# The first loads, the attention mask and the end of attention in a one-core network kernel: three edits at once

## The chip, the cores and the metric

The kernel runs on one core of a Trainium2 chip. The metric is the device time of one execution in microseconds, the median over the runs made. TensorE (PE) multiplies, VectorE (DVE), ScalarE (ACT) and GpSimd (POOL) do elementwise work, SyncE (SP) only issues transfers; ACT and POOL issue some as well. The engines run their own lists of instructions in order and meet at semaphores.

## The reference, cut to what matters

The input is x, 64 sequences of 64 tokens with 256 features, and one type (0 to 2) per sequence.

```python
def gated(x, wi0, wi1, wo): return gelu(x @ wi0) * (x @ wi1) @ wo       # 256 -> 1024 -> 256
# first network: a shared one and one chosen by type, mixed by a gate per sequence
y = mix(gated(x, Wi0[t], Wi1[t], Wo[t]), gated(x, sWi0, sWi1, sWo))
x = x + attention(y, 16 heads of 16, causal, softmax) @ Wo + bo
# second network: three shared relu networks, two experts by type, mixed by a gate of four
z = mix(experts(x), relu(x @ s0) @ t0, relu(x @ s1) @ t1, relu(x @ s2) @ t2)
x = x + moe(z)      # router of three layers, top 2 of 8 experts with a capacity
```

## The kernel before, in words

Every float32 product is split: data and weights are each held as a float16 high part and a float16 low part, and three float16 matmuls (high by high, high by low, low by high) add up to the product. So each matrix that is used must be loaded, scaled to a high part by ACT (`first_weights`, `weight_high`) and to a low part by DVE, and so must each piece of x (`x_group`).

The stages follow one another: the shared gated network `cs` (4 iterations of 16 steps), the typed gated network `ce`, attention over 16 chunks of 256 tokens, three shared relu networks `es[0]` to `es[2]`, the experts `ee`, the router, the experts of the last layer, and the output. Attention is a software pipeline written out by hand: its loop variable i runs to NA + 1 = 17, and in pass i every engine works on chunk i (scores), i - 1 (probabilities by V) and i - 2 (output product, residual sum `x1`). In the last two passes there is little left to do.

Start. DVE works out an order of the sequences by type (up to L1720, semaphore `perm`); SP and POOL wait for it, since which sequence is loaded where depends on it. Then SP issues sequences 0, 2, 4, 6 of the first group (L551), POOL 1, 3, 5, 7 (L451); SP then issues the third matrix `c_swo` (L598) and 8 more sequences, and POOL the first two typed matrices (L446). ACT's list is: high parts of matrices 0 and 1 (L1327), high part of x (L1336), high part of matrix 2 (L1327), and then the steps of the network (gelu L1384, copy L1386). DVE's list is the low parts in the same order (L1725, L1731), then per step the product (L1944) and the low part (L1946). Five blocks of small instructions stand between DVE's steps 2 to 6 of iteration 0: `chunk_tables`, `pair_weights`, `identities`, `masks`, `bias_scale`. On PE a step is `first` (L848, 12 matmuls of 512 columns here) two steps ahead of `second` (L868, 6 matmuls), and `second` of a step waits for DVE's low part of that step.

Attention. `scores` (L973, L979) writes, for each half r of a chunk, a causal mask into two banks of PSUM by one matmul each with the 128 x 128 identity, and adds 8 matmuls with a contraction of 64 rows, which stand in pairs on rows 0 to 63 and 64 to 127. The row maxima (L2064) are turned and subtracted in a second, turned product (L997, L1008). The last three waits of PE are for denominators (L1024), their turning (L1033, after POOL's L476) and the output product (L773, after DVE's L2091).

End of attention. SP loads the rows of x for the residual into one buffer `xin` and can only reload it when DVE's `x1` of the chunk before is made (L657). ACT adds the bias to it (L1500), DVE makes `x1` (L2109), ACT (L1517, L1518) and POOL (L490) split it. `es[0]` starts with three `first` steps, and `second` of its step 0 waits for `x1` of the last chunk (L861); ACT does not touch `es[0]` before POOL has split the last chunk (L1520).

Of the kernel before, what the change touches and what calls it, by code (L numbers as in the profile page):

```python
# [18 lines left out]
ALU = mybir.AluOpType  # L19
# [57 lines left out]
def build(nc, a):  # L77
    ctx = ExitStack()
    with ctx:
# [19 lines left out]
        identb = sb("identb", [128, 128], BF16)  # L99
        upper = sb("upper", [128, 128], F32)  # L100
# [53 lines left out]
        def y_of(c):  # L154
            return y_early[c] if c < 2 else y[:, c % 3]

# [59 lines left out]
        def dp(unit, h):  # L216
# [45 lines left out]
            "w_first_in0", "w_first_in1", "w_first_in2", "w_first_hi", "w_first_lo", "w_in0", "w_in1", "w_hi", "w_ready", "x_half", "x_in0", "x_in1", "x_hi", "x_lo",  # L262
# [171 lines left out]
        def _(pool):  # L434
# [14 lines left out]
            for j in range(1, 8, 2):  # L449
                b = pool.value_load(tbl[0:1, ds(j + T_PERM, 1)], min_val=0, max_val=B - 1)  # L450
                pool.dma_start(xf[:, 0, :, j * S:(j + 1) * S],  # L451
                               a["x"][ds(b, 1)].rearrange("b p (k n) -> p (b k) n", k=KC)).then_inc(s["x_half"], 16)
# [90 lines left out]
        def _(sp):  # L543
            sp.dma_start(itok_i, a["itok"]).then_inc(s["small_in"], 16)
            sp.dma_start(gate_vec, a["gv"].partition_broadcast(128)).then_inc(s["small_in"], 16)
            sp.dma_start(first_stage[0], a["c_swi0"]).then_inc(s["w_first_in0"], 16)
            sp.wait_ge(s["perm"], 1)
# [5 lines left out]
            def g_is_first(g, u):  # L553
                return isinstance(g, int) and g == 0 and u == 0

            def x_group(g, u, fresh=False):

                if not fresh:
                    sp.wait_ge(s["x_lo"], g * 2 + (u - 1))
                for j in range(0, 8, 2 if g_is_first(g, u) else 1):  # L560
                    load_x(xf[:, u, :, j * S:(j + 1) * S], g * 16 + (8 * u + j)).then_inc(s[f"x_in{u}"], 16)
# [13 lines left out]
            def stores(p):  # L575
# [19 lines left out]
                if p is cs:  # L595

                    x_group(0, 0, True)
                    sp.dma_start(first_stage[2], a["c_swo"]).then_inc(s["w_first_in2"], 16)  # L598
# [56 lines left out]
            def xin_load(c):  # L655
                if c >= 1:
                    sp.wait_ge(s["x1"], c)  # L657
                for j in range(GB):
                    load_x(xin[:, :, j * S:(j + 1) * S], c * GB + j).then_inc(s["xin_in"], 16)
# [7 lines left out]
            for i in range(0, NA + 2):  # L667
# [56 lines left out]
        def _(pe):  # L724
# [66 lines left out]

            def ffn(p):
                if p is cs:
                    pe.wait_ge(s["perm"], 1)
                else:
# [3 lines left out]
                if p is es[0]:  # L799
                    pe.wait_ge(s["exp"], 2 * NA)  # L800
# [14 lines left out]
                def weight(off, half, matrix, part, col):  # L815
                    if not p.dynamic:
                        return w16(p.slots[matrix], part, col)
                    base = (p.slots + matrix + (2 * half if p.two_experts else 0)) * SLOT + part * MAT + col
                    return arena.bitcast(U8)[:, ds(off * 2 + base * 2, 256)].bitcast(F16)

# [6 lines left out]

                def parts(place):

                    if isinstance(place, list):  # L830
                        return [(off, start, h * CP, CP) for h, (start, off) in enumerate(place)]
                    return [(*place, 0, p.n)]

                def first(i, st, place):

                    half, f = divmod(st, FC)
                    if p is cs and f == 0:
                        pe.wait_ge(s["x_lo"], i * 2 + (half + 1))
                    if p is es[0] and f == 0:
                        pe.wait_ge(s["x1_lo"], i * 4 + (2 * half + 2))  # L840
                    for g in range(2 if p.gated else 1):
                        if p is cs and isinstance(i, int) and i == 0 and st == 0:
                            pe.wait_ge(s["w_first_lo"], g + 1)
                        bank, col = p.bank(st, g)
                        for off, start, c0, width in parts(place):
                            for k in range(KC):
                                for n, (wp, xp) in enumerate(SPLIT):
                                    last = mm(ps[:, bank, col + c0:col + c0 + width], weight(off, half, g, wp, k * F + f * 128),  # L848
                                              xh[:, xp, k, ds(start, width)],
                                              start=(k == 0 and n == 0), stop=(k == KC - 1 and n == 2))  # L850
                    last.then_inc(p.l1, 1)

                def second(i, st, place):
# [6 lines left out]
                    if p is es[0] and isinstance(i, int) and i == 0 and st == 0:  # L860
                        pe.wait_ge(s["x1"], NA)  # L861
# [3 lines left out]
                    for m in range(2):  # L865
                        for off, _start, c0, width in parts(place):
                            for n, (wp, hp) in enumerate(SPLIT):
                                last = mm(ps[:, 4 + 2 * half + m, c0:c0 + width],  # L868
                                          weight(off, half, 2 if p.gated else 1, wp, f * D + m * 128),
# [5 lines left out]
                def body(i, lastone, pair=None, to_pair=False):  # L875
# [9 lines left out]
                    for st in range(n_st):  # L885
# [5 lines left out]
                        second(i, st, place[st // FC])  # L891
                        if p is ee and isinstance(i, int):
# [31 lines left out]
                        if nxt < n_st:  # L924
                            first(i, nxt, place[nxt // FC])
# [1411 lines left out]
```

## Time and profile before

| | us |
|---|---|
| median of 3 runs | 2384.69 |
| lowest and highest | 2378.08 and 11851.42 |
| the profiled execution | 2383.66 |
| span of its instructions | 2382.1 |

The busy shares of the span are PE 96%, DVE 48%, ACT 45%, POOL 14%, and the mean granted clock of TensorE is 0.989 of full speed. Outside the span lie 1.6 us. A share of the whole span says little about the few places that the change touches; those are read from the timeline of each engine.

### The profile page before, as it was taken

The page shows a single profiled execution, that of the slowest core. Times are in us where ns is not written, and L with a number is a line of the kernel's source. Part 1 is how long each engine was busy: PE and PEld are TensorE (multiplying, and loading weights), DVE is VectorE, ACT ScalarE, POOL GpSimd, SP SyncE. Part 2 cuts the span into 40 slices and gives each one's busy share as a digit, 9 for nine tenths or more (in the row PEclk, how much of TensorE's full clock was granted, in tenths as well). Part 3 has the DMA queues.
Part 4 walks back from the last instruction along what each step waited for, and adds up shares of the span by engine and source line. Part 5 has one row for each costly group of instructions (what it writes and reads, how often), then busy time and mean ns, then how long its engine had stood idle before and what let it go on. Part 6 is the DMA issues. An engine that isn't in the chain of part 4 may idle for free.

```text
span 2382.1 us, 52351 instructions
## 1 busy us (share of the span) xinstructions
PE 2298.1 (96%) x19309; PEld 1488.7 (62%) x19328; DVE 1139.5 (48%) x2330; ACT 1081.7 (45%) x2070; POOL 330.0 (14%) x488
## 2 busy tenths in 40 slices
PE   5999999999999799999999999999999999989998
PEld 2444488887787344444444888888544444458886
DVE  5554355445899342332332544545344444444444
ACT  3554345444777442332332444433344444446663
POOL 0000000011564100000000111110000000004556
PEclk9999999999999899999999999999999999999999
DMA  4231111012443330121110323342211111012434
GB/s 125 82 104 53 36 50 35 18 33 68 103 107 87 117 120 35 45 80 45 45 44 31 111 102 115 115 151 77 76 36 36 35 35 35 35 44 70 127 97 127
DMA packets 165381, 171.94 MB, mean 72 GB/s; under 512 B 98964, under 2 KB 142996, under 8 KB 156244
## 3 DMA queue, kind: packets, MB, share of 16 engines
q1 hardware_dynamic: 139012, 80.22, 11.6%
q0 software_dynamic: 21232, 74.24, 9.3%
q10 hardware_dynamic: 4960, 15.05, 2.1%
q8 instruction: 120, 1.97, 0.4%
q14 instruction: 57, 0.47, 0.1%
HBM read 107.57 MB, written 50.86 MB: 67 GB/s over the span
## 4 chain that ended last, share of the span: by engine, by line
PE 93%; DVE 3%; ACT 1%; issue 1%; DMA 1%; SPq 1%; POOL 0%; POOLq 0%; DVEq 0%
PE ps L848 32%; PE ps L868 25%; PE ps L1139 14%; PE ps L1258 4%; PE ps L1270 4%; PE ps L1128 3%; PE ps L773 3%; PE ps L997 1%; PE ps L1054 1%; PE ps L1008 1%; PE ps L973 1%; PE ps L1153 1%; PE ps L1045 1%; PE ps L1024 1%; PE ps L744 0%
## 5 line engine op out<-in xcount | busy, mean ns | idle before, releaser
L848 PE MATMUL ps<-xh,arena 128*128 (+1 forms) x5376 | 890.8, 308 | 18.4 <-DVE xh L1731 10.3
L868 PE MATMUL ps<-misc,arena 128*128 128x256 f16 (+2 forms) x4128 | 715.0, 309 | 19.6 <-DVE misc L1950 9.6
L848 PEld LDWEIGHTS ps<-xh,arena 128*128 (+1 forms) x5376 | 515.7, 98 | 290.8 <-issue 29.7
L868 PEld LDWEIGHTS ps<-misc,arena 128*128 (+1 forms) x4128 | 395.2, 98 | 234.4 <-issue 19.9
L1950 DVE SCALAR_TENSOR_TENSOR misc<-ps,misc 128x256 f16<-128x256 f32 (+1 forms) x464 | 248.0, 535 | 494.1 <-ACT misc L1388 492.2
L1388 ACT ACTIVATE misc<-ps 128x256 f16<-128x256 f32 (+1 forms) x464 | 218.7, 472 | 523.9 <-PE ps L848 522.6
L1139 PE MATMUL ps<-arena 128*128 128x512 f16 x1536 | 337.2, 379 | 0.0
L1139 PEld LDWEIGHTS ps<-arena 128*128 128x128 f16 x1536 | 148.0, 98 | 172.8
L2194 DVE TENSOR_TENSOR arena<-misc,arena 128x512 f16<-128x512 f32 x128 | 88.6, 692 | 229.3 <-ACT arena L1537 229.3
L1944 DVE TENSOR_TENSOR arena<-ps,misc 128x256 f32<-128x256 f32 (+1 forms) x200 | 101.7, 508 | 141.9 <-ACT misc L1384 141.2
L1536 ACT ACTIVATE misc<-ps,bias 128x512 f32<-128x512 f32 x128 | 87.7, 685 | 172.7 <-PE ps L1139 162.8
L1384 ACT ACTIVATE misc<-ps 128x256 f32<-128x256 f32 (+1 forms) x200 | 90.2, 451 | 163.4 <-PE ps L848 163.4
L1386 ACT ACTIVATE misc<-arena 128x256 f16<-128x256 f32 (+1 forms) x200 | 96.9, 485 | 131.2 <-DVE arena L1944 131.2
L1946 DVE TENSOR_TENSOR misc<-arena,misc 128x256 f16<-128x256 f32 (+1 forms) x200 | 103.6, 518 | 110.1 <-ACT misc L1386 110.1
L404 POOL DMA_DIRECT2D xh<-misc x120 | 59.4, 501 | 572.0 <-DVE misc L2245 569.5
L1258 PE MATMUL ps<-arena 128*128 128x384 f16 (+1 forms) x768 | 124.9, 299 | 1.0 <-ACT arena L1584 1.0
L1270 PE MATMUL ps<-arena,misc 128*128 128x256 f16 x960 | 125.6, 273 | 0.1
L2251 DVE TENSOR_TENSOR misc<-misc 128x256 f16<-128x256 f32 (+1 forms) x128 | 62.8, 491 | 107.8 <-ACT misc L1604 107.8
L1270 PEld LDWEIGHTS ps<-arena,misc 128*128 128x128 f16 x960 | 93.8, 98 | 17.9 <-DVE misc L2251 0.6
L1603 ACT ACTIVATE misc<-ps,bias 128x256 f32<-128x256 f32 (+1 forms) x128 | 67.3, 525 | 70.5 <-PE ps L1258 70.0
L520 POOL DMA_DIRECT2D parts_d<-misc x64 | 43.1, 674 | 374.5 <-DVE misc L1830 368.3
L1258 PEld LDWEIGHTS ps<-arena 128*128 128x128 f16 x768 | 75.1, 98 | 23.7 <-ACT arena L1584 1.2
(305 smaller groups left out, 2062.1 us busy)
## 6 DMA issues: line engine op xcount, KB each, us to landing
wstage<-in_m_w POOLq DMA_DIRECT2D x16, 1024.0 KB, 5.7
parts_d<-misc POOLq DMA_DIRECT2D x64, 256.0 KB, 2.5
arena<-src_d SPq DMA_DIRECT2D x64, 256.0 KB, 3.6
src_d<-misc SPq DMA_DIRECT2D x24, 512.0 KB, 3.1
arena<-parts_d ACTq DMA_DIRECT2D x12, 1024.0 KB, 8.0
wstage<-in_c_wi POOLq DMA_DIRECT2D x6, 1024.0 KB, 5.6
wstage<-in_r_w POOLq DMA_DIRECT2D x5, 1024.0 KB, 5.4
cshare_d<-misc SPq DMA_DIRECT2D x8, 512.0 KB, 3.1
```

Of the source, the lines that this page charges most:

```text
L848: last = mm(ps[:, bank, col + c0:col + c0 + width], weight(off, half, g, wp, k * F + f * 128), xh[:, xp, k, ds(start, width)], start=(k == ...
L868: last = mm(ps[:, 4 + 2 * half + m, c0:c0 + width], weight(off, half, 2 if p.gated else 1, wp, f * D + m * 128), hid[:, st % 4, hp, c0:c0 ...
L1139: last = mm(ps[:, 4 + fo % 2, :], w16(R_W2[k // 2], wp, (k % 2) * F + fo * 128), h1[:, k, xp, :], start=(k == 0 and n == 0), stop=(k == FC ...
L1258: last = mm(ps[:, (e * 16 + st) % 3, 0:n], w16(MOE_W[e % 2][0], wp, k * F + f * 128), xe[:, xp, k, e * PER_E + c0:e * PER_E + c0 + n], sta ...
L1270: last = mm(ps[:, 3 + t, 0:D], hid[:, st % 4, hp, i_t * 128:(i_t + 1) * 128], w16(MOE_W[e % 2][1], wp, f * D, D), start=(f == 0 and j == 0 ...
L1384: fn(p.gbuf(st), ps[:, bank, col:col + p.n], ACT.Gelu_apprx_tanh, scale=1 / SH).then_inc(p.g, 1)
L1386: fn(hid[:, st % 4, 0, 0:p.n], p.fbuf(st), ACT.Copy).then_inc(p.hi, 1)
L1388: fn(hid[:, st % 4, 0, 0:p.n], ps[:, bank, col:col + p.n], ACT.Relu).then_inc(p.hi, 1)
L1944: v.tensor_tensor(p.fbuf(st), src, p.gbuf(st), ALU.mult).then_inc(p.mul, 1)
L1946: v.tensor_tensor(hid[:, st % 4, 1, 0:p.n], p.fbuf(st), hid[:, st % 4, 0, 0:p.n], ALU.subtract).then_inc(p.h, 1)
L1950: v.scalar_tensor_tensor(hid[:, st % 4, 1, 0:p.n], src, 0.0, hid[:, st % 4, 0, 0:p.n], ALU.max, ALU.subtract).then_inc(p.h, 1)
L2194: v.tensor_tensor(dst[:, 1, :], gt[:, (st % 2) * 512:(st % 2 + 1) * 512], dst[:, 0, :], ALU.subtract).then_inc(s["r_lo"], 1)
```

## The change

1. Start. `c_swo` is issued by SP before the wait for `perm`. The first eight sequences are issued by three queues (SP 0, 3, 6; ACT 1, 4, 7, after its wait for `perm` and behind the high parts of matrices 0 and 1; POOL 2, 5), and their high and low parts are made in two halves of 256 columns. ACT makes the high part of matrix 2 ahead of those of x, and runs one gelu on a column that nobody needs. `chunk_tables` moves ahead of the first step of DVE, the other blocks are spread over steps 2 to 8.
2. Mask. The two mask matmuls of a half have 64 rows each, one on rows 0 to 63 and one on 64 to 127, with a table `twin` that holds the identity twice side by side.
3. End of attention. The three `first` steps of `es[0]` go between PE's last products of attention; ACT's and DVE's `hidden` for step 0 go into pass 16; the output product of the last chunk goes behind `second` of step 0, its `x1` behind `hidden` of step 1 on DVE, its high part behind `hidden` of step 2 on ACT. The residual rows of the last two chunks go to the buffer `ex`, which lies unused by then, so that they need not wait for `x1`; ACT adds the bias to both ahead of the copy of the denominators (`rden`).

```diff
+        X_IN = (B // 16 * 128 - 128, B // 16 * 128)
+        def xin_of(c):
+            return ex[:, c % 2] if c >= NA - 2 else xin
+        FIRST_SP, FIRST_ACT, FIRST_POOL = (0, 3, 6), (1, 4, 7), (2, 5)
+        def first_x(queue, j, arrived):
+            b = queue.value_load(tbl[0:1, T_PERM + j:T_PERM + j + 1], min_val=0, max_val=B - 1)
+            queue.dma_start(xf[:, 0, :, j * S:(j + 1) * S], a["x"][ds(b, 1)].rearrange("b p (k n) -> p (b k) n", k=KC)
+                            ).then_inc(s[f"{arrived}{j // 4}"], 16)
...
@@ SP
             sp.dma_start(first_stage[0], a["c_swi0"]).then_inc(s["w_first_in0"], 16)
+            sp.dma_start(first_stage[2], a["c_swo"]).then_inc(s["w_first_in2"], 16)
             sp.wait_ge(s["perm"], 1)
...
             def xin_load(c):
-                if c >= 1:
+                if c >= NA - 2:
+                    sp.wait_ge(s["y_lo"], c + 1)
+                elif c >= 1:
                     sp.wait_ge(s["x1"], c)
...
-                if 0 <= i - 1 < NA:
+                if 0 <= i - 1 < NA - 2:
                     xin_load(i - 1)
                 if 0 <= i - 2:
                     x1_store(i - 2)
+                if NA - 2 <= i < NA:
+                    xin_load(i)
@@ PE
-                    mm(ps[:, 2 * r + hpp, :], identb[:, :], causal[:, :, :].rearrange("p h n -> p (h n)"), start=True, stop=False,
-                       skip_group_check=True)
+                    rows = slice(64 * hpp, 64 * hpp + 64)
+                    mm(ps[:, 2 * r + hpp, :], twin[rows, :, :].rearrange("p g n -> p (g n)"),
+                       causal[rows, :, :].rearrange("p h n -> p (h n)"), start=True, stop=False, skip_group_check=True)
...
+                if i == NA:
+                    pe.wait_ge(s["w_ready"], es[0].need_w)
+                    pe.wait_ge(s["exp"], 2 * NA)
+                    first(es[0], 0, 0, (0, 0))
...
+                if i == NA:
+                    first(es[0], 0, 1, (0, 0))
                 if 0 <= i - 1 < NA:
                     normalisers_turned(i - 1)
...
+                if i == NA:
+                    first(es[0], 0, 2, (0, 0))
...
                     if p is es[0] and isinstance(i, int) and i == 0 and st == 0:
+                        pe.wait_ge(s["norm"], 2 * NA)
+                    if p is es[0] and isinstance(i, int) and i == 0 and st == FC:
                         pe.wait_ge(s["x1"], NA)
...
+                        if p is es[0] and isinstance(i, int) and (i, st) == (0, 0):
+                            pe.wait_ge(s["o_lo"], NA)
+                            output_product(NA - 1)
@@ ACT
-            x_group(0, 0)
+            act.wait_ge(s["perm"], 1)
+            for j in FIRST_ACT:
+                first_x(act, j, "x_first")
             first_weights(2)
+            act.wait_ge(s["x_first0"], 48)
+            act.wait_ge(s["x_pool0"], 16)
+            fn(xh[:, 0, :, 0:256], xf[:, 0, :, 0:256], ACT.Copy, scale=SX).then_inc(s["x_first_hi"], 1)
+            act.wait_ge(s["x_first1"], 48)
+            act.wait_ge(s["x_pool1"], 16)
+            fn(xh[:, 0, :, 256:512], xf[:, 0, :, 256:512], ACT.Copy, scale=SX).then_inc(s["x_hi"], 1)
+            fn(small[:, 231:232], pidx[:, :], ACT.Gelu_apprx_tanh)
...
+                if i == NA:
+                    act.wait_ge(s["x_in0"], X_IN[0] + 64)
+                    x_bias(NA - 2)
+                    act.wait_ge(s["x_in1"], X_IN[1] + 64)
+                    x_bias(NA - 1)
...
+                if i == NA:
+                    act.wait_ge(s["p_lo"], 2 * NA)
+                    hidden(es[0], 0, 0)
@@ DVE
+            chunk_tables()
...
+                v.tensor_tensor(twin[:, :, :], ident[:, 0:64].unsqueeze(1).to_broadcast([128, 2, S]),
+                                ident[:, 64:128].unsqueeze(1).to_broadcast([128, 2, S]), ALU.add)
...
+                        if p is es[0] and isinstance(i, int) and (i, st) == (0, 1):
+                            x1_make(NA - 1)
...
+                if i == NA:
+                    hidden(es[0], 0, 0)
```

## Rows read from the trace of the kernel before

**Rows 1.** Part 4 of the page: the chain that ended last, by engine.
```profile
PE 93%; DVE 3%; ACT 1%; issue 1%; DMA 1%; SPq 1%; POOL 0%; POOLq 0%; DVEq 0%
```

**Rows 2.** PE in the first 62 us: start, length, line, count, wait before.
```profile
22.30 7.76 PE L848 MATMUL ps<-xh,arena 128*128 128x512 f16 x24 [10.28 <-DVE xh L1731]
33.25 1.96 PE L868 MATMUL ps<-misc,arena 128*128 128x512 f16 x6 [3.19 <-DVE misc L1946]
...
54.50 2.74 PE L868 MATMUL ps<-misc,arena 128*128 128x512 f16 x6 [2.73 <-DVE misc L1946]
...
60.08 1.46 PE L868 MATMUL ps<-misc,arena 128*128 128x512 f16 x6
61.38 2.75 PE L848 MATMUL ps<-xh,arena 128*128 128x512 f16 x12
```

**Rows 3.** Two stretches: length, busy by engine and count, PEclk, DMA share, GB/s.
```profile
22.30:60.08 37.78, 30.90 (x114) 12.38 (x115) 22.07 (x72) 12.11 (x16) 0.00 (x0) 0.91 0.34 102
41.60:45.65 4.05, 4.05 (x20) 1.86 (x19) 3.50 (x27) 0.60 (x1) 0.00 (x0) 1.00 0.22 49
```

**Rows 4.** ACT in the first 30 us.
```profile
10.39 1.91 ACT L1327 ACTIVATE arena<-arena 128x2048 f16<-128x2048 f32 x1 [0.62 <-DMA arena<-in_c_swi]
19.88 1.06 ACT L1336 ACTIVATE xh<-misc 128x1024 f16<-128x1024 f32 x1 [7.58 <-DMA misc<-in_x]
26.88 1.91 ACT L1327 ACTIVATE arena<-arena 128x2048 f16<-128x2048 f32 x1 [5.94 <-DMA arena<-in_c_swo]
```

**Rows 5.** DVE's low part of the third matrix.
```profile
28.82 2.29 DVE L1725 SCALAR_TENSOR_TENSOR arena<-arena 128x2048 f16<-128x2048 f32 x1 [6.62 <-ACT arena L1327]
```

**Rows 6.** SP's four issues of x, and POOL's two issues of matrices.
```profile
13.42 4.59 SPq L551 DMA_DIRECT2D misc<-in_x  x4
18.26 1.10 POOL L446 DMA_DIRECT2D wstage<-in_c_wi  x2
```

**Rows 7.** Loads of x, issue to landing: those of 13 to 18.5 us, those of 24 to 30 us.
```profile
DMA to landing us min/median/max: 2.2/2.3/2.8
...
DMA to landing us min/median/max: 2.7/4.0/5.4
```

**Rows 8.** PE in one pass of attention.
```profile
666.04 0.60 PE L973 MATMUL ps<-causal,identb 128*128 128x512 bf16 x2
666.58 0.40 PE L979 MATMUL ps<-arena 64*128 64x128 f16 x8
...
669.04 1.47 PE L773 MATMUL ps<-arena 128*128 128x256 f16 x12
...
671.39 0.84 PE L997 MATMUL ps<-arena 64*128 64x128 f16 x24
672.16 1.07 PE L1008 MATMUL ps<-shift,arena 128*128 128x128 bf16 x16
```

**Rows 9.** One whole pass of attention, columns as in rows 3.
```profile
665.34:677.63 12.29, 12.03 (x295) 9.77 (x295) 11.62 (x19) 10.12 (x19) 7.64 (x7) 1.00 0.46 107
```

**Rows 10.** PE at the end of attention and the start of the next stage.
```profile
777.18 0.95 PE L1024 MATMUL ps<-small,arena 128*128 128x2 f16 x32 [1.22 <-DVE arena L2060]
779.59 1.11 PE L1033 MATMUL ps<-ident,arena 128*128 128x128 f32 x4 [1.46 <-POOL arena L476]
780.51 2.75 PE L773 MATMUL ps<-arena 128*128 128x256 f16 x12
...
787.01 1.49 PE L773 MATMUL ps<-arena 128*128 128x256 f16 x12 [2.33 <-DVE arena L2091]
...
800.83 2.72 PE L868 MATMUL ps<-misc,arena 128*128 128x512 f16 x6 [8.45 <-DVE misc L1950]
```

**Rows 11.** ACT at the end of attention.
```profile
795.22 0.91 ACT L1500 ACTIVATE arena<-arena,bias 128x256 f32<-128x256 f32 x2 [9.09 <-DMA arena<-in_x]
```

**Rows 12.** SP's loads of the residual rows of chunks 13 and 15.
```profile
764.36 4.58 SPq L551 DMA_DIRECT2D arena<-in_x  x4
...
784.74 4.70 SPq L551 DMA_DIRECT2D arena<-in_x  x4
```

More of the change, by code:

```diff
@@ L448, in _ @@
             pool.wait_ge(s["perm"], 1)
[L449 to L452, printed above, removed]
+            for j in FIRST_POOL:
+                first_x(pool, j, "x_pool")
             for i in range(14):
@@ L790, in value_bias, with weight, parts, first @@
                 last.then_inc(s["bv_mm"], 1)
+            def weight(p, off, half, matrix, part, col):
+                if not p.dynamic:
+                    return w16(p.slots[matrix], part, col)
+                base = (p.slots + matrix + (2 * half if p.two_experts else 0)) * SLOT + part * MAT + col
+                return arena.bitcast(U8)[:, ds(off * 2 + base * 2, 256)].bitcast(F16)
+            def parts(p, place):
+                if isinstance(place, list):
+                    return [(off, start, h * CP, CP) for h, (start, off) in enumerate(place)]
+                return [(*place, 0, p.n)]
+            def first(p, i, st, place):
+                half, f = divmod(st, FC)
+                if p is cs and f == 0:
+                    pe.wait_ge(s["x_lo"], i * 2 + (half + 1))
+                if p is es[0] and f == 0:
+                    pe.wait_ge(s["x1_lo"], i * 4 + (2 * half + 2))
+                for g in range(2 if p.gated else 1):
+                    if p is cs and isinstance(i, int) and i == 0 and st == 0:
+                        pe.wait_ge(s["w_first_lo"], g + 1)
+                    bank, col = p.bank(st, g)
+                    for off, start, c0, width in parts(p, place):
+                        for k in range(KC):
+                            for n, (wp, xp) in enumerate(SPLIT):
+                                last = mm(ps[:, bank, col + c0:col + c0 + width], weight(p, off, half, g, wp, k * F + f * 128),
+                                          xh[:, xp, k, ds(start, width)],
+                                          start=(k == 0 and n == 0), stop=(k == KC - 1 and n == 2))
+                last.then_inc(p.l1, 1)
             def ffn(p):
@@ L813, in at_chunk @@
                     return off, first
[L815 to L819, printed above, removed]
                 def pair_place():
@@ L826, in pair_place @@
                             for at_off in ((T_OFFE if p.two_experts else T_OFFC),)]
[L828 to L851, printed above, removed]
                 def second(i, st, place):
@@ L934, in ffn @@
                     carry(place0)
-                for st in range(p.lead):
-                    first(0, st, place0)
+                for st in range(p.lead if p is not es[0] else 0):
+                    first(p, 0, st, place0)
                 body(0, False)
@@ L1415, in body @@
                     for st in range(p.last_steps if lastone else 16):
-                        hidden(i, st)
+                        if not (p is es[0] and isinstance(i, int) and (i, st) == (0, 0)):
+                            hidden(p, i, st)
+                        if p is es[0] and isinstance(i, int) and (i, st) == (0, 2):
+                            x1_high(NA - 1)
                         if st == 1 and not first:
@@ L1480, in v_high, with x_bias @@
                 last.then_inc(s["v_hi"], 1)
+            def x_bias(c):
+                for k in range(KC):
+                    last = fn(xin_of(c)[:, k, :], xin_of(c)[:, k, :], ACT.Identity, bias=ab[:, 3, k:k + 1])
+                last.then_inc(s["xb"], 1)
             for i in range(0, NA + 2):
@@ L1496, in _ @@
                     gate_exp(2, 2, HB)
-                if 0 <= i - 2 < NA:
+                if 0 <= i - 2 < NA - 2:
                     act.wait_ge(s["xin_in"], (i - 1) * 64)
-                    for k in range(KC):
-                        last = fn(xin[:, k, :], xin[:, k, :], ACT.Identity, bias=ab[:, 3, k:k + 1])
-                    last.then_inc(s["xb"], 1)
+                    x_bias(i - 2)
+                if i == NA:
[3 more added lines that the diff above has]
+                    x_bias(NA - 1)
                 if 0 <= i < NA:
```

175 lines of the change are left out of this document (97 added, 78 removed).

## The prediction

> **What bounds the kernel now.** I read the chain of waits first. It is TensorE (PE) for 93% of the span [rows 1], so a microsecond is won where PE waits, or where it does the same work slowly or needlessly. Then I read PE's timeline with the wait in front of each group. The change touches three places where PE is not at its best. In the first 60 us it starts at 22.30, then waits 3.19 and 2.73 us for DVE's low part, and the first `second` after the latter takes 2.74 us, where the undisturbed one takes 1.46 [rows 2]. In a pass of attention it is busy for 12.03 of 12.29 us [rows 9]. From 776 to 806 us it waits four times, 13.46 us together, and works at half speed in between: 12 matmuls of 256 columns take 2.75 us where they take 1.47 in a pass [rows 8, 10].
>
> **Start, what is taken away.** From 22.30 to 60.08 PE does 114 matmuls of 512 columns in 37.78 us [rows 3]. Six of them at full clock take 1.30 (60.08 to 61.38) [rows 2], so 114 take 24.7; 13.1 us are lost. Of these the first 24 lose 2.6 (7.76 against 5.2), which is the slow beginning and stays. The other 10.5 are the two waits (5.9), the slow stretches behind them and a shorter wait. The first wait comes from the third matrix: ACT can make its high part at 26.88 only, when `c_swo` lands, and the gelu of step 0 stands behind it on ACT, DVE's low part (28.82, 2.29 us) in front of DVE's product [rows 4, 5]. The second comes from the blocks of small instructions on DVE; the tables alone take 4.05 us [rows 3].
>
> **Start, what comes.** `c_swo` is issued some 16 us earlier and has landed long before ACT is free, at about 12 us. It shares the transfer with the second matrix, whose high part now starts at 10.39; behind two queues' worth of data I give it 10.4 to 12. ACT then issues its three sequences. Four take SP 4.59 us, 1.15 each, and they land 2.3 us after issue, under two large loads 4.0 in the median and 5.4 at most [rows 6, 7]. So ACT's last is issued at about 16.5 to 17.5 and lands at 19 to 23, since POOL, with two x loads fewer, issues its two large loads about 2.2 us earlier than 18.26 [rows 6]. Before, x was there at 19.88 [rows 4]. I take 20.5. The two halves of the high and low parts add half of 1.06 and half of DVE's; PE starts at about 22.8, half a microsecond later than now. DVE then makes the low part of matrix 2 (2.29, to 24.9) and the tables (4.05, to about 29), which now stand in front of its product of step 0. That product was due at about 27.5, so the tables are not wholly hidden: `second` of step 0 starts near 31.1, 0.6 us after PE has run out of `first`. From there 90 matmuls take 19.5, to 50.6, against 60.08. The remaining blocks are now at most about 2 us in a step of 3.9 us, of which DVE's own work is some 1.4, so they are covered; if that cover fails it costs tenths. The gelu table load (ACT is idle then) and `twin`, one more instruction of about 0.2 us, are covered too. **Gain 9.5**, bounds 5 (x at 24 us) and 11.
>
> **Mask.** A pair of mask matmuls occupies PE for 0.54 us (666.04 to 666.58). I have no 64-row pair of 512 columns in the trace. The nearest rows are the 24 matmuls of L997, 64 rows and 128 columns each, which take 0.84 us, against 1.07 for 16 of the same columns with all rows (L1008) [rows 8]: 35 ns against 67, so two row halves do run side by side, at 0.52 of the price. That gives 0.28 for the pair and 0.26 saved, 32 times, 8.3 us of PE. The bounds are 0 (a long pair does not overlap) and 0.32 saved each, 10 us. The pages on the chip have a rule here. The Trainium skill, TensorEngine Tiling, Key Properties, says that a change of the tiling mode drains TensorE; by it the mask, now in the mode of the products behind it, would also save drains, and the term would lie at its upper bound. No row here separates a drain.
> What is late next is DVE: it is busy for 11.62 of the 12.29 us [rows 9]. With 0.5 taken from PE's pass, PE needs about 11.8, DVE 11.6 and a few waits on ACT. So I count 0.4 a pass for 13 steady passes and nothing in the first two and the last. **Gain 5.5**, bounds 0 and 8.5.
>
> **End of attention.** PE's four waits are 1.22, 1.46, 2.33 and 8.45 [rows 10], 13.46 in all. Half speed costs 0.5 at L1033, 1.3 at L773 and 0.4 behind it, and 1.3 and 1.0 at 800.83 and its successor, 4.5 together; 18 us can be had. The three `first` steps are 6 matmuls each, 1.30 us, and fit the first three waits: the first covers 1.22, the second 1.46 but for 0.2, the third stands in front of the wait for the denominators. What ends the last wait now is the residual load: SP may issue it only after `x1` of chunk 14, at 784.74, and ACT can add the bias only at 795.22 [rows 11, 12]. In the new order SP is done with chunk 13 at 769 (764.36 and 4.58) [rows 12], stores `x1`, and issues chunk 14 at about 771 to 775.6, then waits for `x1` of chunk 13, stores it, and issues chunk 15 from about 777.5 to 782. It lands near 783.7 (2.3 us after the last issue, no large load is near; POOL's stand behind `x1` of chunk 14).
> **The new wait** is on ACT: the bias of chunk 15 stands in front of `rden`. Queued behind it are `rden`, `hidden` of step 0, the high part of chunk 14 and the high part of the output; DVE's normalised output waits for `rden`, and with it DVE's `hidden`. With 0.9 for the bias, 0.6 for `rden`, 0.7 and 0.7 for DVE's two, `second` of step 0 starts near 786.7, while PE has run out at about 784.1: 2.6 us of waiting. The output product of the last chunk follows after another 0.3, and its `x1` is behind the steps. So 3 us of waits stay and perhaps 1 us of slow work behind them. **Gain 14**, bounds 10 (chunk 15 lands like the x loads under large ones, 3 later, and half speed follows) and 16.5.
>
> **The sum** is 9.5 + 5.5 + 14 = 29. The profiled execution took 2383.66, so 2354.7, call it 2355. The median of the runs is 1 us above the profiled execution, but one of the three runs lies at 2378, so the median of the runs after can be off by 5. All three stages end before PE-bound stages (cs, then es), so nothing later takes the gain back; the number of steps there is unchanged.
>
> **Rivals.**
> *The mask gives nothing*, because a long pair runs one after the other, or because DVE, at 11.62 of 12.29 us, holds the pass: 2360. For it: DVE's share. Against it: the 24 short matmuls.
> *x comes late at the start.* ACT's three loads sit behind two ACT copies and under POOL's two large loads; x at 24 us makes PE start near 26, and only the waits behind are won: start gain 5, total 2359. The Trainium skill, DMA: Bandwidth & Descriptors, Rules for kernel authors, says that spreading loads over queues saves issue time alone, since they share the same 16 engines; by that the three queues bring x no sooner than 19.88, which is near what I took.
> *Several of these together*, with a slow stretch at the end of attention: 2366.
> *Slower: the clock falls inside attention.* If the shortened pass makes PE wait for DVE in each pass, and half speed follows each wait as it follows those of rows 10, a pass loses some 1.3 us on each group of 12 wide matmuls, 2.5 in all, 14 times 35 us, and the mask gives nothing: 2383.7 - 23.5 + 35 = 2395. It decides from about 10 of 14 passes on. Against it: the waits would be of 0.1 to 0.3 us, those of rows 10 were over 1.2, and the pass of rows 9 with its 0.26 us of idle PE has clock 1.00.
> *More than forecast*: everything at its upper bound, 2348.
>
> **How the numbers follow.** Chances: forecast 0.50, mask nothing 0.15, x late 0.15, several together 0.12, more 0.05, slower 0.03. The range must take in the last but one cases and the spread of 5 between runs: 2344 to 2370. Two per cent, about what a measurement of this kernel can tell from no change, is 48 us, so even the best sum (36) lies within it, and so do all rivals: within 2% 0.94, faster 0.03, slower 0.03.
>
> **What the profile after would show.** Right: PE's first L848 at 22 to 24 us and no wait over 1 us behind it up to 100 us; the state of 60.08 reached at about 50.6; the mask pair at about 0.28 us and passes of 11.8 to 11.9; in the last pass `first` of `es[0]` between L1024, L1033 and L773, one wait of 2 to 3 us before the first `second`, and PEclk 1.00 there but for one dip. Wrong: x landing after 23 us; a mask pair still at 0.5; passes still at 12.3 with DVE idle nowhere; ACT waiting for residual rows beyond 785 us.

## The result and the profile after

| | before | after |
|---|---|---|
| median of the runs made together | 2383.15 us (4 runs) | 2359.49 us (4 runs, 2358.76 to 2362.12) |
| profiled execution | 2383.66 us | 2358.76 us |
| span of its instructions | 2382.1 us | 2357.2 us |

The ratio is 0.9905, with a 95% interval of 0.9892 to 0.9917. The kernel is about 24 us faster, 1% of its time. One of the four runs before took 11851.42 us, which nothing here explains; the other three lie between 2378.08 and 2384.69.

The two profiled executions differ by 24.9 us. To find where, I took points of PE's timeline that both kernels pass, and compared their times. Line numbers have moved: `first` is L833 now (L848 before), `second` L883 (L868), the mask L992 (L973), the scores L998 (L979), the output product L788 (L773).

| stretch | reached before | reached after | gained in the stretch |
|---|---|---|---|
| to the sixth `second` of `cs` | 60.08 | 55.02 | 5.1 |
| to the first mask of attention | 572.31 | 565.38 | 1.9 |
| to the first mask of the last pass of scores | 765.45 | 751.87 | 6.6 |
| to the steady steps of `es[0]` | 805.69 | 778.87 | 13.2 |
| to the start of `ee` | 1302.21 | 1275.39 | 0.0 |
| to the end | 2382.1 | 2357.2 | -1.9 |

In the kernel before, the trace has no record of the first of the two mask matmuls at either mask point (it shows x1 where there are two), so 572.31 and 765.45 are 0.2 late. With that put right the gains are 1.7 to the first mask, 6.6 in the passes and 13.5 at the end of attention; these are used below.

**The start.** PE's timeline of the changed kernel. The columns are those of [rows 2].

```profile
27.41 8.14 PE L833 MATMUL ps<-xh,arena 128*128 128x512 f16 x24 [15.23 <-DVE xh L1790]
35.59 1.46 PE L883 MATMUL ps<-misc,arena 128*128 128x512 f16 x6
...
55.02 1.46 PE L883 MATMUL ps<-misc,arena 128*128 128x512 f16 x6
```

Against [rows 2] all waits behind the first one are gone, and so are the slow steps behind them: each step takes 3.89 us. But PE starts at 27.41, not at 22.30. ACT's timeline and the transfers of x tell why.

```profile
17.24 1.91 ACT L1354 ACTIVATE arena<-arena 128x2048 f16<-128x2048 f32 x1 [2.30 <-issue]
19.06 0.61 ACT L1386 ACTIVATE xh<-misc 128x512 f16<-128x512 f32 x1
25.96 0.63 ACT L1389 ACTIVATE xh<-misc 128x512 f16<-128x512 f32 x1 [6.29 <-DMA misc<-in_x]
```

The issues in the window 15.2 to 17.3 us, first of x on SP, then of x on ACT, then of the two typed matrices on POOL, each with the time to its landing:

```profile
L430 SPq DMA_DIRECT2D misc<-in_x x2: 542/542/543, 15.1 to 16.4; - x2
DMA to landing us min/median/max: 2.2/5.1/8.0
...
L430 ACTq DMA_DIRECT2D misc<-in_x x2: 551/554/557, 15.4 to 16.6; - x2
DMA to landing us min/median/max: 2.4/5.8/9.3
...
L460 POOL DMA_DIRECT2D wstage<-in_c_wi x2: 543/554/564, 16.2 to 16.7; - x2
DMA to landing us min/median/max: 6.2/7.6/8.9
```

The third matrix is done on ACT by 19.1, as expected. The first half of x is there too. The last sequence of SP and the last of ACT are issued at 16.4 and 16.6, in between POOL's two loads of 1024 KB at 16.2 and 16.7. They hold 64 KB each, and take 8.0 and 9.3 us where the ones a microsecond earlier take 2.2 and 2.4. ACT waits 6.29 us for them.

It is not the place between the two that matters. SP goes on with the next eight sequences of 64 KB, issued from 17.7 to 26.8 us:

```profile
DMA to landing us min/median/max: 2.1/3.8/7.5
```

One by one, those issued at 17.7, 19.0, 20.2, 21.5 and 22.9 take 7.5, 6.5, 5.4, 4.4 and 3.3 us. All land at 25.2 to 26.2, and the two late ones of the first group at 24.4 and 25.9; the large loads have landed by 25.6 (16.7 and 8.9). So each small load issued while the large ones are in flight lands at about the time when these are done. The trace of the kernel before shows the same. Its large loads are issued at 18.3 and 18.8 and take 8.8 and 10.9; the four loads of x issued next, from 19.4 to 23.3, take:

```profile
DMA to landing us min/median/max: 6.4/7.8/9.3
```

**The passes of attention.** PE at the end of one pass and at the start of the next:

```profile
616.39 1.53 PE L1073 MATMUL ps<-arena 128*64 128x128 f16 x48
617.85 0.39 PE L992 MATMUL ps<-causal,twin 64*128 64x512 bf16 x2
618.08 0.39 PE L998 MATMUL ps<-wstage 64*128 64x128 f16 x8
618.30 0.38 PE L992 MATMUL ps<-causal,twin 64*128 64x512 bf16 x2
```

The next group starts 0.22 us after a mask pair (0.54 in [rows 8]). More than the masks has become shorter. Two mask matmuls with all rows would take 0.43 at the rate of six in 1.30, so 0.11 of the 0.54 was something else. The group of scores (L979 before, L998 now) does the same work in both. Yet from its start to that of the second mask pair it is 0.33 us before (665.71 below, 666.04 in [rows 8]) and 0.22 now:

```profile
665.40 0.38 PE L973 MATMUL ps<-causal,identb 128*128 128x512 bf16 x1 [0.16 <-issue]
665.71 0.40 PE L979 MATMUL ps<-arena 64*128 64x128 f16 x8
```

Both read as 0.11 us for each change between a tile of 64*128 and one of 128*128. That is an estimate from these differences. Three such changes a pass are gone and one is left, behind the last scores: 3 x 0.11 and twice 0.43 - 0.22 make 0.75. The stretch of twelve passes, as in [rows 3], and a pass in which PE is never idle:

```profile
606.43:751.87 145.44, 140.04 (x3617) 119.15 (x3614) 139.15 (x217) 120.65 (x214) 87.73 (x68) 1.00 0.46 104
643.16:654.59 11.43, 11.43 (x305) 9.87 (x303) 11.11 (x18) 9.37 (x18) 7.19 (x6) 1.00 0.46 103
```

Such a pass now takes 11.43 us. The shortest of before took 12.17, so 0.74 is saved. The twelve passes together took 151.38 before; they gained 5.9. Twelve times 0.74 would be 8.9. The other 3 us are in passes of 12.7 to 14.2 us, about two of them where PE stops for what the trace calls "issue". All of PE's waits from 600 to 752 us (total, times, longest):

```profile
PE ps L1073 <- issue: 3.2, 5, 0.8
PE ps L992 <- issue: 2.2, 2, 1.3
PE ps L788 <- issue: 0.4, 1, 0.4
PE ps L788 <- DVE arena L2181: 0.2, 1, 0.2
```

The kernel before has such stops as well. From 606 to 766 us they are 5.7 us in 19 places, 14 of them in front of the mask (L973), 3.3 us together with a longest of 1.2; the other 13 are thus 0.16 each. These 13 are no stops. Each stands, as at 665.40 above, where one of the two mask matmuls has no record. In end_only2 (below), which keeps the old mask and has both records, the gap isn't there, and the shortest pass takes 12.18 all the same. In the twelve passes the real stops are then 3.2 us before and 5.1 now.

How much of the 6.6 us is the mask? From the first mask of attention to that of the last pass, the three traces with the old mask take 193.1 (before), 193.8 (start_only) and 194.3 us (end_only2). The six with the new one take 186.5 (after, bias_later), 188.6 (late_fetch), 188.8 (both_fixes), 189.3 (mask_only) and 189.5 (tables_back). The difference of the means is 5.6 us, and one trace can be off by 2.

**The end of attention.** PE from the last pass on, to be laid beside [rows 10]:

```profile
763.67 1.47 PE L833 MATMUL ps<-xh,arena 128*128 128x512 f16 x6
765.79 0.95 PE L1043 MATMUL ps<-small,arena 128*128 128x2 f16 x32 [0.65 <-DVE arena L2137]
766.60 1.46 PE L833 MATMUL ps<-xh,arena 128*128 128x512 f16 x6
...
769.12 1.47 PE L788 MATMUL ps<-arena 128*128 128x256 f16 x12 [0.27 <-DVE arena L2181]
...
771.50 1.47 PE L833 MATMUL ps<-xh,arena 128*128 128x512 f16 x6
774.42 1.46 PE L883 MATMUL ps<-misc,arena 128*128 128x512 f16 x6 [1.46 <-DVE misc L2011]
776.25 1.48 PE L788 MATMUL ps<-arena 128*128 128x256 f16 x12 [0.37 <-DVE arena L2177]
777.57 1.46 PE L833 MATMUL ps<-xh,arena 128*128 128x512 f16 x6
```

Waits of 13.46 us have become 2.75, and no product in these rows is at half speed. One short slow stretch is left ahead of them, at 757 us, where the 16 matmuls of L1027 take 1.89 us instead of 1.07. ACT shows what the one long wait is for:

```profile
765.54 0.91 ACT L1532 ACTIVATE arena<-arena,bias 128x256 f32<-128x256 f32 x2
771.36 0.91 ACT L1532 ACTIVATE arena<-arena,bias 128x256 f32<-128x256 f32 x2 [4.92 <-DMA arena<-in_x]
772.29 0.60 ACT L1562 ACTIVATE arena<-ps 128x512 f32<-128x512 f32 x1
```

It is the bias of chunk 15 (the second L1532), for which ACT waits 4.92 us, while `rden` (L1562), which needs nothing of it, is queued behind.

**Given back.** At the start of `ee` both kernels wait 2.82 us for "issue". Before, the first 18 matmuls behind it took 2.25 us; after, 3.83. At the start of `ce`, behind a wait of 2.86 in both, it is the other way round: 5.88 us for 36 matmuls before, 4.19 after.

```profile
283.76 4.19 PE L833 MATMUL ps<-xh,arena 128*128 x36 [2.86 <-issue]
...
1275.39 3.83 PE L833 MATMUL ps<-xh,arena 128*128 x18 [2.82 <-issue]
```

So 1.7 us of the 24.9 came from a place that the change doesn't touch, and 1.6 went at another. The last 0.3 of the table I haven't traced.

### The profile page after: what moved, and what is told of

Its sections match the earlier page's. It is cut to its first block, busy times and chain, and to the rows that moved or that the text cites. A ratio compares the mean times of both kernels' runs of the same rounds, so it can differ in the third digit from the quotient of the medians.

```text
span 2357.2 us, 52378 instructions
## 1 busy us (share of the span) xinstructions
PE 2284.8 (97%) x19327; PEld 1486.6 (63%) x19328; DVE 1140.3 (48%) x2332; ACT 1083.5 (46%) x2072; POOL 328.5 (14%) x486
## 4 chain that ended last, share of the span: by engine, by line
PE 94%; DVE 1%; DMA 1%; ACT 1%; issue 1%; SPq 1%; POOL 0%; ACTq 0%; POOLq 0%; DVEq 0%
PE ps L833 33%; PE ps L883 26%; PE ps L1166 14%; PE ps L1285 4%; PE ps L1297 4%; PE ps L1155 4%; PE ps L788 3%; PE ps L1016 1%; PE ps L1073 1%; PE ps L1180 1%; PE ps L1027 1%; PE ps L1064 1%; PE ps L1043 0%; DMA misc<-in_x 0%; PE ps L978 0%
## 5 line engine op out<-in xcount | busy, mean ns | idle before, releaser
L833 PE MATMUL ps<-xh,arena 128*128 (+1 forms) x5376 | 888.8, 308 | 23.4 <-DVE xh L1790 15.2
L883 PE MATMUL ps<-misc,arena 128*128 128x256 f16 (+2 forms) x4128 | 712.0, 308 | 5.9 <-DVE misc L2011 2.6
L833 PEld LDWEIGHTS ps<-xh,arena 128*128 (+1 forms) x5376 | 514.6, 98 | 292.6 <-issue 30.3
L883 PEld LDWEIGHTS ps<-misc,arena 128*128 (+1 forms) x4128 | 394.9, 98 | 218.9 <-issue 5.5
```

Source lines behind the costliest of these rows:

```text
L833: last = mm(ps[:, bank, col + c0:col + c0 + width], weight(p, off, half, g, wp, k * F + f * 128), xh[:, xp, k, ds(start, width)], start=(k ...
L883: last = mm(ps[:, 4 + 2 * half + m, c0:c0 + width], weight(p, off, half, 2 if p.gated else 1, wp, f * D + m * 128), hid[:, st % 4, hp, c0: ...
```

## The experiments

Each ratio is to runs of the kernel before that were made together with those of the experiment. The kernels were measured in several groups, whose medians of the kernel before lie between 2382.33 and 2384.14, so a difference between medians of two groups is good to about 2 us at best. The edits are shown shortened. Where I speak of an anchor below, it is the sixth `second` of `cs` at the start (60.08 before, 55.02 after) or the steady step of `es[0]` (805.69, 778.87).

**Each of the three parts alone.** The kernel before, with one of the numbered parts of the change.

start_only:

```diff
# the kernel before, and:
+            sp.dma_start(first_stage[2], a["c_swo"]).then_inc(s["w_first_in2"], 16)   # ahead of the wait for perm
+                    for j in FIRST_SP:  first_x(sp, j, "x_first")      # ACT and POOL likewise
...
+            chunk_tables()                                             # ahead of DVE's first step
```

The other blocks spread over steps 2 to 8 and the early gelu are in it as well.

> Only the edits at the start. Theory (the gains add up, and the start gives what its timeline shows, 5 us, since the last two loads of x land late): 2378 us, PE's first product near 27.4 us, the six products at 60.1 before are reached at 55.0. Rival (the start gives the 9.5 us forecast, and the loss is elsewhere): 2374 us. A chance dip of the clock at a fixed spot can add or remove 1.7 us.

mask_only:

```diff
-                    mm(ps[:, 2 * r + hpp, :], identb[:, :], causal[:, :, :]...)
+                    rows = slice(64 * hpp, 64 * hpp + 64)
+                    mm(ps[:, 2 * r + hpp, :], twin[rows, :, :]..., causal[rows, :, :]...)
```

> Only the 64-row masks. Theory: a mask pair takes 0.22 us in place of 0.54 and a pass about 11.9 in place of 12.3; 6 to 7 us less, 2377 us. Rival (DVE holds the pass): a pass stays over 12.1 and the gain is under 3 us, 2381 us.

end_only2:

```diff
+                if i == NA:  first(es[0], 0, 0, (0, 0))                # and steps 1 and 2 further down
...
+                if c >= NA - 2:
+                    sp.wait_ge(s["y_lo"], c + 1)                       # residual rows into ex
```

ACT's and DVE's parts of the third edit are in it too. Only `X_IN[0]` differs from the changed kernel (64 higher), since the old start counts its first four loads of x on the same semaphore.

> Only the edits at the end of attention (the count that ScalarE waits for fitted to the loads of the kernel before). Theory: 13 to 14 us less, 2370 us, with one wait of about 1.5 us before the first second product. Rival (part of the gain at the end came from the shortened passes in front): under 11 us less.

| | median (range), us | ratio, 95% interval | below the kernel before |
|---|---|---|---|
| start_only | 2377.63 (2374.74 to 2380.6) | 0.9976 (0.9967 to 0.9986) | 5.8 |
| mask_only | 2375.71 (2373.9 to 2379.43) | 0.997 (0.9959 to 0.9981) | 7.7 |
| end_only2 | 2372.38 (2369.34 to 2374.73) | 0.9957 (0.9943 to 0.9971) | 11.8 |

The sum is 25.3 us and the whole change gave 23.7. Each interval is over 2 us wide to either side, so no interaction shows; one of several us could hide. The trace of mask_only gains 3.9 us in the passes, half of what the medians show; its shortest pass takes 11.42 and the mean of its last twelve 12.3, not the 11.9 expected. The rival (under 3 us) is out by the medians. start_only shows the same fault as the whole change:

```profile
28.03 6.79 PE L852 MATMUL ps<-xh,arena 128*128 128x512 f16 x24 [15.75 <-DVE xh L1749]
36.21 1.46 PE L872 MATMUL ps<-misc,arena 128*128 128x512 f16 x6 [1.39 <-DVE misc L1965]
```

It reaches its anchor at 55.63, 4.45 us earlier than before. In end_only2 the wait in front of the first `second` is 3.13 us, twice what was expected. 17.5 us are gained up to the anchor at 788.20. Of these 4.8 had been gained ahead of attention, at places that the edit doesn't touch, and 1.2 of them were lost again in the passes: 13.9 came from the end itself, so the rival (under 11) is out.

**late_fetch: is it POOL's large loads that hold up x?** The changed kernel, with POOL's first two fetches behind the landing of x.

```diff
             for j in FIRST_POOL:
                 first_x(pool, j, "x_pool")
+            pool.wait_ge(s["x_first0"], 48)
+            pool.wait_ge(s["x_first1"], 48)
             for i in range(14):
                 fetch(i)
```

> The changed kernel, but GpSimd issues its two large loads only when the loads of x by SyncE and ScalarE have landed. Theory (the large loads make the last two loads of x land 8.0 and 9.3 us after issue): these land 2.3 us after issue, at about 19 us, PE's first product starts near 20.8 in place of 27.4, and 6 us are won over the changed kernel, 2353 us. Rival (they are slow because of the loads queued on their own queues, or the queues' number): x still lands after 24 us and nothing is won. Second rival (the tables on DVE then hold the first step): half of it, 3 us.

Measured: 2355.27 us (2352.83 to 2357.45), ratio 0.9882 (0.9862 to 0.9903). First the issues of x in the window 15.2 to 17.3 us, all within 0.2 us of those of the changed kernel, and the landing of the loads that POOL, SP and ACT issue there, then ACT, then PE:

```profile
L430 SPq DMA_DIRECT2D misc<-in_x x2: 543/543/543, 15.2 to 16.5; - x2
L430 ACTq DMA_DIRECT2D misc<-in_x x2: 551/554/557, 15.5 to 16.7; - x2
...
DMA to landing us min/median/max: 2.3/2.4/2.9
```

```profile
19.64 0.61 ACT L1391 ACTIVATE xh<-misc 128x512 f16<-128x512 f32 x1
```

```profile
21.16 7.22 PE L835 MATMUL ps<-xh,arena 128*128 128x512 f16 x24 [8.82 <-DVE xh L1792]
29.34 1.46 PE L885 MATMUL ps<-misc,arena 128*128 128x512 f16 x6 [0.96 <-DVE misc L2009]
...
45.50 1.47 PE L885 MATMUL ps<-misc,arena 128*128 128x512 f16 x6 [0.46 <-DVE misc L2009]
```

The same two issues at the same time now land after 2.4 (SP) and 2.8 us (ACT). The only edit is the later issue of the large loads, at 20.1 instead of 16.2. So the large loads are the cause, and the lateness of ACT's issues or the number of queues is not. PE starts 6.25 us earlier than in the changed kernel and is 5.6 ahead at the anchor, near the 6 expected. A wait of 0.96 shows for DVE's tables, which the late x had hidden. Of the 5.6 us, 4.3 are left at the first mask of attention (561.06 against 565.38), the rest being lost at the start of `ce`, where 36 matmuls take 5.48 us instead of 4.19. Another 2.1 are lost in the passes of attention, which the edit doesn't touch. In the spans 1.8 are left, in the medians 4.2.

**tables_back: are the tables hidden where they stand?** late_fetch with `chunk_tables` back at step 2 of `cs`.

```diff
-            chunk_tables()
...
+                                chunk_tables()
```

> late_fetch with the tables for all chunks made at step 2 of the first network, as in the kernel before, so that the start of late_fetch is kept and the third of the start's edits is undone. Theory (the tables are hidden before the first product when they stand in front of the steps, and cost where they stand in the steps): the 4 us of table work fall between the subtractions of the steps; TensorE, which needs one subtraction in each 3.9 us, waits 1.5 to 2.7 us once behind step 2, and the state that late_fetch reaches at its time plus nothing comes that much later; the whole is 2 to 4 us slower than late_fetch, near 2358. Rival (VectorE has room for them in the steps, since its part of a step is shorter than TensorE's): no wait of TensorE over 0.5 us behind step 2, the time within 1 us of late_fetch's 2355.3.

Measured: 2360.48 us (2358.84 to 2361.24), ratio 0.9903 (0.9887 to 0.992), 5.2 us above late_fetch by the medians; the two intervals overlap. PE and DVE:

```profile
28.66 1.46 PE L885 MATMUL ps<-misc,arena 128*128 128x512 f16 x6 [0.30 <-DVE misc L2007]
...
43.51 1.47 PE L885 MATMUL ps<-misc,arena 128*128 128x512 f16 x6 [3.03 <-DVE misc L2007]
```

```profile
35.37 0.15 DVE L1797 COPY misc<-misc 128x1 f32<-128x1 f32 x1
...
41.37 0.69 DVE L2005 TENSOR_TENSOR arena<-ps,misc 128x512 f32<-128x512 f32 x1
```

Six microseconds of small instructions lie in front of the product of step 3: the tables from 35.37 to 39.3, and behind them, to 41.37, the gate vectors and `pair_weights`, which late_fetch has at this step as well. PE waits 3.03 us for the product. The rival is out. With the tables in front of the steps PE waits 0.96 and 0.46; with them among the steps, 0.30 and 3.03, and the anchor comes at 51.29 against 49.39, 1.9 later. That is the low end of the 2 to 4 expected. The spans differ by 3.7 us and the medians by 5.2; the rest came in stretches that the edit doesn't touch, and I don't credit it to the tables.

**bias_later: the bias in front of rden.** The changed kernel, with the bias of chunk 15 behind the work that doesn't need it.

```diff
-                    act.wait_ge(s["x_in1"], X_IN[1] + 64)
-                    x_bias(NA - 1)
...
+                # behind rden, hidden(es[0], 0, 0), the high part of x1 of chunk 14 and that of the output of chunk 15
+                if i == NA + 1:
+                    act.wait_ge(s["x_in1"], X_IN[1] + 64)
+                    x_bias(NA - 1)
```

> The changed kernel, but ScalarE adds the bias to the rows of chunk 15 in the pass after, behind the copy of the denominators, the hidden part of step 0 and the two high parts. Theory (the wait for those rows in front of the copy of the denominators is what holds the first second product): the copy comes at about 768.5 in place of 772.3, PE's wait of 1.46 us is gone, 1.5 us won; the next things late are the rows themselves, which hold only x1. Rival (the output of the probabilities, or PE itself, is as late): under 0.5 us.

Measured: 2357.78 us (2355.0 to 2361.25), ratio 0.9899 (0.9882 to 0.9915). PE and ACT:

```profile
772.93 1.46 PE L883 MATMUL ps<-misc,arena 128*128 128x512 f16 x6
...
775.55 1.46 PE L833 MATMUL ps<-xh,arena 128*128 128x512 f16 x6
```

```profile
768.78 0.60 ACT L1560 ACTIVATE arena<-ps 128x512 f32<-128x512 f32 x1 [2.50 <-PE ps L1052]
```

`rden` starts 3.5 us earlier and both waits of PE (1.46 and 0.37) are gone. The next `first` comes at 775.55 instead of 777.57, 2.0 us earlier, of which 0.1 was there ahead of the first wait. The median is 1.7 lower, which the intervals alone wouldn't tell from nothing; the trace does.

**both_fixes: the two together.**

> The late large loads at the start and the later bias together. Theory (they add up): 6 and 1.5 us less than the changed kernel on the timeline, 2352 us; the stretches of half clock, which fall on other waits in each kernel, can take or give 2 us of it.

Measured: 2353.24 us (2352.74 to 2353.43), ratio 0.9874 (0.9858 to 0.9891). This interval lies, if only just, wholly below that of the change as made (0.9892 to 0.9917), and its median is 6.3 us lower, the lowest here; it overlaps with those of late_fetch and bias_later. Its steady step of `es[0]` comes at 773.66 instead of 778.87, 5.2 us earlier where 7.5 were expected: it is 5.8 ahead at the first anchor, loses 3.8 up to the last pass of attention and wins 3.2 at the end.

**mask_gone: what bounds a pass now?** The changed kernel without the mask matmuls of the first scores. The scores from which the row maxima are taken are then not masked; everything else is computed.

```diff
-                for hpp in range(2):
-                    rows = slice(64 * hpp, 64 * hpp + 64)
-                    mm(ps[:, 2 * r + hpp, :], twin[rows, :, :]..., causal[rows, :, :]...)
...
-                                      start=False, stop=True, ...)
+                                      start=(b2 == 0 and m == 0), stop=True, ...)
```

> The changed kernel without the mask in the first scores: it leaves out the masking of the scores from which the row maxima are taken. It shows what bounds a pass once the mask costs nothing. If PE still bounds it: 0.44 us less a pass, 6 to 7 us in all, 2353 us. If DVE (11.6 us busy in a pass of 12.3 before) now bounds it: passes as in the changed kernel, waits of PE for DVE in each pass, under 2 us less.

Measured: 2356.71 us (2355.24 to 2358.58), ratio 0.9891 (0.9875 to 0.9908). PE's waits from 600 to 752 us:

```profile
PE ps L788 <- DVE arena L2177: 3.4, 8, 0.5
...
PE ps L788 <- DVE arena L2192: 1.0, 4, 0.3
```

PE now waits for DVE in front of the output product 12 times, 4.4 us in all, where it did once. But where it doesn't wait, a pass is as much shorter as the two pairs cost:

```profile
642.79 0.62 PE L994 MATMUL ps<-wstage 64*128 64x128 f16 x16
...
653.78 0.70 PE L994 MATMUL ps<-arena 64*128 64x128 f16 x16
```

That one takes 10.99 us against 11.43. The others of the twelve take 11.2 to 13.6. From the first pass to the last it is 184.2 us, 2.3 less than in the changed kernel and 4.0 less than the mean of the six traces with the new mask, where 0.44 a pass would make 6.6; the median is 2.8 lower. So neither branch came true. In the changed kernel PE still holds the pass (one wait of 0.2 us for DVE in twelve), but DVE is close behind and takes back a good part of any further cut.

## Why the prediction was right, and where it was not

The time came at 2359.5 against a forecast of 2355, inside the range of 2344 to 2370. That it is so near the forecast of 29 us less is in part luck: one term fell short by 4.4, and 1.7 us that came at the start of `ce`, with no term for them, went again behind attention. By the terms:

- **Start, 9.5 forecast, 5.1 measured: the step that failed.** What it says of the waits was right: `c_swo` was done when ACT was free, both waits of [rows 2] and the slow stretches behind them went, the blocks were covered. The step "So ACT's last is issued at about 16.5 to 17.5 and lands at 19 to 23 ... I take 20.5" was wrong in its last part: issued at 16.6, it landed at 25.9. The prediction's own sign of being wrong, "x landing after 23 us", came true. The durations of 4.0 and 5.4 [rows 7] belong to loads issued 6 to 11 us after the first large one, when the large ones were nearly done. The right rows stood in the same trace: loads issued 1 to 5 us behind the large ones take 9.3 to 6.4 us. I had seen that POOL's loads move forward by 2.2 us and counted it as nothing but an upper end. late_fetch shows that they are the cause; there PE starts at 21.16, better than the 22.8 forecast.
- "x late" was among the rivals, with PE starting "near 26" and a gain of 5, and that is the one that came, PE starting at 27.41. Its total of 2359 is hit by luck: by the prediction's own lengths a start at 26 reaches the state of 60.08 at 26 + 7.8 + 19.5 = 53.3, a gain of 6.8, not 5.
- **The second matrix.** Its high part was given 10.4 to 12 and started at 13.03. ACT's first load of x goes out 0.3 us after SP's (13.94 against 13.60), so it cost the loads of x little. No run moves `c_swo` alone.
- The rule of the Trainium skill that stood beside this rival (DMA: Bandwidth & Descriptors, Rules for kernel authors: more queues save issue time alone) agrees with the trace. SP needs 3.29 us for three issues instead of 4.59 for four, and in late_fetch, where nothing large is in the way, ACT takes up the last of x at 19.64, without a wait, against 19.88 with two queues. The estimate "no sooner than 19.88" was of the right size, but a bound on one side only. No run keeps the two queues with the other edits of the start.
- **The tables**: forecast to hold up the first `second` by 0.6 us. In the changed kernel they didn't, since x was late for other reasons and PE's slow first 24 matmuls lasted until 35.55. In late_fetch, where x is on time, it is 0.96, and in start_only 1.39.
- **Mask, 5.5 forecast, 6.6 in this trace, 5.6 by the means of all traces.** The pair takes 0.22, not 0.28, and the changes between tiles of 64 and of 128 rows, which the sum had not priced, cost about 0.11 each. A pass without a stop is 0.74 shorter where I counted 0.4; the stops for "issue" took the rest back, and the sum had no term for them. So the total is right partly by two errors that cancel. "What is late next is DVE" was right, but it begins a little later than I put it: mask_gone reaches it. The rival that the mask gives nothing is out (mask_only, 7.7).
- The rule on changes of the tiling mode (the Trainium skill, TensorEngine Tiling, Key Properties) put the term at its upper bound of 0.32 a pair. The trace agrees: 0.54 became 0.22, and the scores in front of the second pair went from 0.33 to 0.22. The 0.11 is told apart by subtraction alone; no run changes only the mode.
- **End of attention, 14 forecast, 13.5 measured.** The new wait on ACT is there as described, 1.46 us instead of 2.6 (3.13 in end_only2). bias_later shows that it is ACT's order, and that it costs 1.9.
- **Slower, because the clock falls in each pass**: nothing of it. The granted clock of the twelve passes is 1.00.
- "Nothing later takes the gain back" was off by 1.6 us at the start of `ee`, and 1.7 came as a present at the start of `ce`. I had no term for either.

What stays open: why small loads land only with the large ones; why PE stops for "issue" for up to 1.3 us in some passes (the sixth and the fourteenth are long in nearly every trace, whatever the edit); and why one wait of 2.8 us is followed by slow matmuls and an equal one in the next kernel is not. No run here changes only that.

## What to carry to other kernels

When small loads that the first product needs are spread over more queues, look at what the queues do next: a large load that moves forward by two microseconds can cost six. Hold it back until the small ones have landed: here that brought PE's first product forward by 6.25 us, while the third queue brought x 0.2 us. When a wait is put on an engine ahead of work that doesn't need it, it costs as soon as anything behind it is on the path, so put it behind. When you take a duration from a trace, take it from a transfer that stands in the same place against its neighbours, and not from a later one of the same kind. And take the parts of a change one by one: here they added up within the noise.

## What the runs showed of the hardware that was not expected

- A load of 64 KB that is issued while two loads of 1024 KB from another queue are in flight lands at about the time when these are done: issued at 16.4, 16.6, 17.7, 19.0, 20.2, 21.5 and 22.9 us it takes 8.0, 9.3, 7.5, 6.5, 5.4, 4.4 and 3.3, the large ones having landed by 25.6. With these held back, it takes 2.3 to 2.8.
- Two matmuls of 512 columns on 64 rows each, one on the upper and one on the lower half, take 0.22 us together, which is the time of one with all rows (1.30 us for six at full clock). A change between tiles of 64*128 and 128*128 costs about 0.11 us, an estimate from this: eight score matmuls take 0.33 in front of a 128-row mask and 0.22 in front of a 64-row one.
- Behind the wait of 2.86 us at the start of `ce`, 36 matmuls took 5.88 us before, 4.19 after and in bias_later, 5.48 in late_fetch, 5.86 in tables_back and 7.03 in start_only. Behind that of 2.82 at the start of `ee`, 18 took 2.25 before, 3.83 after and in late_fetch, 3.80 in tables_back (wait of 2.65), 2.22 in start_only and 2.28 in bias_later. mask_gone, which has the code of the changed kernel up to attention, took 5.77 at the first place where that took 4.19. So this is noise of 1 to 3 us on any change of this kernel, and it does not go with the edit.
- A gap in a timeline can be a matmul whose record is missing: 0.16 us "idle" in front of a group that shows x1 where there are two.
